# Feed-forward part of a gated cross-attention block: two unit tiles of the next batch beside each token tile of this one

## The chip, the cores and the metric
The kernel runs on one core of a Trainium2 chip, on five engines with queues of their own: TensorE (PE, and PEld for its weight loads), VectorE (DVE), ScalarE (ACT), GpSimd (POOL) and SyncE (SP), which issues the transfers. Each engine works through its queue in order; the queues meet only at semaphores. The metric is the device time of one launch in microseconds, lower is better, as the median of several runs.

## The reference, cut to what matters
There are 4 batches of 1024 tokens with 512 features. After a gated cross-attention (unchanged here) comes a gated feed-forward part:

```
x = x + tanh(g_ffn) * ffn(layernorm(x))

h = bit_linear(x, w1)            # 512 -> 2048 hidden units
h = depthwise_conv1d(h)          # three taps along the tokens, per unit
h = silu(h + conv_b)
y = bit_linear(h, w2)            # 2048 -> 512

bit_linear(x, w): xq = round(x * 127 / max|x|) / scale, one scale per token, over all its features
                  wq = ternary weights;  return xq @ wq.T
```

What matters for the order of the work: the rounding before the second product needs the largest |h| of a token over all 2048 units. So no token of a batch can go on to the second product before all units of that batch are done. The convolution, the other way round, needs neighbouring tokens of one unit.

## The kernel before, in words
The sizes: a batch has NT = 8 token tiles of 128 tokens, and KH = 16 unit tiles of 128 hidden units. The first product is made with units on the partitions and 1024 tokens along the row; the second with tokens on the partitions. PSUM has 8 banks of 512 words; a unit tile takes two of them (a pair), a turned unit tile two more (banks 6 and 7).

For unit tile n (counted through the batches), these steps run; the letters are used in the rest of this document:
- F(n): 8 matmuls of the first product (`pe_first`, L1745) into a pair of banks.
- g(n): VectorE multiplies the pair in place by the tokens' scales (`dve_scaled`, L1263).
- t(n), u(n): ScalarE writes the middle tap with its bias (L1008) and the last tap (L1012), both from the pair (`taps`).
- c(n): VectorE adds the first tap, from the pair (`first_tap`, L1489). The pair is free after it.
- tap(n): GpSimd adds the last tap (L819).
- C(n): 8 transposes to tokens on the partitions, into banks 6 and 7 (`turn_units`, L1889).
- silu(n): ScalarE writes the activated unit tile from there into `hT`, a tile of 8 tokens by 2048 units in fp32 that holds one batch (L1045).
- max(n): VectorE takes the largest value of each token (`biggest`, L1494).

When the 16 unit tiles of a batch are done, five small VectorE operations give the scales (`unit_scales`, L1498 to L1505). Then for token tile m:
- VectorE rounds it in place, by adding a large constant (`round_up`, L1511 and L1513); ScalarE subtracts the constant into bf16 (`integers`, L1018 and L1023).
- T(m): 16 transposes (`turn_h`, L1876) into two banks; ScalarE copies them out (`turned_units`, L1054 for halves, L1030 for a whole one).
- S(m): 16 matmuls of the second product (`second`, L1902).
- o(m): VectorE scales the result and adds it to x (`add_out`, L1518); SyncE stores it.

So each batch has a stage of units and then a stage of token tiles. Only the first few unit tiles of the next batch are begun within the token stage: F, g and the taps for four of them. Three pairs of banks rotate among the unit tiles, and two of them are lent to the token stage (`PAIR`, `out_bank`, `turned_bank`). The order is written out by hand in four loops, one per engine, and the waits count named events (`D_DVE`, `D_ACT`).

In the gaps stands a second chain: the layernorm and rounding of the last batch's x, done by VectorE in the token stages of batches 0 and 1 (`ln_steps`, from L1072 to L1125), with one ScalarE square root (L824), and the transposes and the row of scales for batches 2 and 3 (`ln_turn`, L1594; `ln_row`, L1580).

Of the kernel before, what the change touches and what calls it, by code (L numbers as in the profile page):

```python
# [18 lines left out]
F32 = mybir.dt.float32  # L19
# [6 lines left out]
P = 128  # L26
# [17 lines left out]
def flamingo_gated_block(nc, x, ctxT, mask, mask_cols, g_x, g_f, wsT, bk_cols, b_v, wtT, bq_cols, woT, b_out,  # L44
# [13 lines left out]
    with ExitStack() as ctx:  # L58
# [156 lines left out]
        hT = sb("hT", [P, NT, HID], F32)  # L215
# [27 lines left out]
        hsc = sb("hsc", [P, NT], F32)  # L243
        hdq = sb("hdq", [P, NT], F32)
# [87 lines left out]
        pool_tap = sem("pool_tap")  # L332
        pe_ct = sem("pe_ct")
# [70 lines left out]
        PAIR = [[j % 3 for j in range(KH)]]  # L404
        for b in range(1, B):
            first_three = PAIR[b - 1][KH - 3:]
            PAIR.append([first_three[j] if j < 3 else first_three[(j - 4) % 3] for j in range(KH)])

        def pair(b, j):
            return ps[:, 2 * PAIR[b][j]:2 * PAIR[b][j] + 2, :].rearrange("p a t -> p (a t)")  # L410

        def out_bank(b, i):
            return 2 * PAIR[b][KH - 3] + i % 2

        def turned_bank(b, i):
# [18 lines left out]
        def counts(names):  # L434
# [8 lines left out]
        LN_DVE, LN_DVE_N = counts([f"stat{i}" for i in range(NT)] + [f"aggr{i}" for i in range(NT)] + ["rstd"]  # L443
                                  + [f"ln{i}" for i in range(NT)] + [f"am{i}" for i in range(NT)]
                                  + ["amc", "rec", "asc", "adq"]
                                  + [f"{w}{i}" for i in range(NT) for w in ("xr", "xi")])
        LN_ACT, LN_ACT_N = counts(["row"] + [f"xT{i}" for i in range(NT // 2)])
        names = ["g0_0", "g0_1"]
        for b in range(B):
            for j in range(KH):  # L450
                if b == 0 or j >= 3:
                    names.append(f"c{b}_{j}")
                if j >= 2:
                    names.append(f"hmax{b}_{j - 2}")
                if j + 2 >= KH and b + 1 < B:
                    names.append(f"g{b + 1}_{j + 2 - KH}")
                elif j + 2 < KH and (b == 0 or j + 2 >= 4):
                    names.append(f"g{b}_{j + 2}")
            names += [f"hmax{b}_{KH - 2}"] + ([f"c{b + 1}_0", f"g{b + 1}_2"] if b + 1 < B else []) + [f"hmax{b}_{KH - 1}"]
            names += [f"{w}{b}" for w in ("hm", "hmc", "hrec", "hsc", "hdq")]  # L460
            names += [f"sc{b}_0a", f"sc{b}_0", f"sc{b}_1"] + ([f"c{b + 1}_1"] if b + 1 < B else [])
            names += [f"sc{b}_2"] + ([f"c{b + 1}_2"] if b + 1 < B else [])
            for i in range(NT):
                if i + 3 < NT:
                    names.append(f"sc{b}_{i + 3}")
                if i == NT - 1 and b + 1 < B:
                    names.append(f"g{b + 1}_3")
                names.append(f"o{b}_{i}")
        D_DVE, _ = counts(names)
        names = ["t0_0", "u0_0", "t0_1", "u0_1"]  # L470
        for b in range(B):
            for j in range(KH):
                if j + 2 >= KH and b + 1 < B:
                    names += [f"t{b + 1}_{j + 2 - KH}", f"u{b + 1}_{j + 2 - KH}"]
                elif j + 2 < KH and (b == 0 or j + 2 >= 3):
                    names += [f"t{b}_{j + 2}", f"u{b}_{j + 2}"]
                names.append(f"silu{b}_{j}")
            if b + 1 < B:
                names += [f"t{b + 1}_2", f"u{b + 1}_2"]
            names += [f"sub{b}_0a", f"sub{b}_0", f"hT{b}_0a"]  # L480
            for i in range(NT):
                if i + 1 < NT:
                    names.append(f"sub{b}_{i + 1}")
                names.append(f"hT{b}_{i}")
        D_ACT, _ = counts(names)

# [34 lines left out]
        def _(sp):  # L521
# [262 lines left out]
        def _(pool):  # L784
# [41 lines left out]
        def act_ln_row(act, b):  # L826
# [1152 lines left out]
```

## Time and profile before

| what | value |
|---|---|
| median of 3 runs | 1693.51 us (1690.1 to 1697.37) |
| the profiled execution's own time | 1691.95 us |
| its span, first to last instruction | 1690.1 us |
| TensorE, share of the span | 94% |
| VectorE | 67% |
| ScalarE | 51% |
| GpSimd | 43% |
| mean granted clock of TensorE | 0.982 |

The span is what the rows below are counted in; the run's own time is 1.85 us longer. The shares are means over stages that differ: attention fills the time to about 1285 us, the feed-forward part what follows. Times of rows are microseconds from the start of the span. Consecutive operations of one engine overlap by about a tenth of a microsecond at their ends, so the start-to-start distance is what an operation costs its engine, and the printed duration is what an operation on another engine waits for.

### The profile page before, as it was taken

How to read it: one execution, taken by the hardware profiler on the slowest of the kernel's cores; microseconds unless marked ns; L12 is line 12 of the kernel's file. 1: busy time of each engine (PE TensorE's matmuls, PEld its weight loads, DVE VectorE, ACT ScalarE, POOL GpSimd, SP SyncE). 2: the span in 40 equal slices, each digit the busy share in tenths (PEclk: the TensorE clock that was granted, in tenths of full speed). 3: DMA queues.
4: the chain of work that ended last, by engine and by line, in shares of the span. 5: the costliest groups of instructions: out<-in, count | busy, mean ns of one | idle time of the engine just before them, and what ended most of it. 6: DMA issues, size and time to landing. Idle time of an engine off the chain costs nothing. (4 is left out here: it accounts for less than half of the span.)

```text
span 1690.1 us, 23527 instructions
## 1 busy us (share of the span) xinstructions
PE 1592.1 (94%) x8370; PEld 1001.8 (59%) x8370; DVE 1130.5 (67%) x2237; ACT 856.5 (51%) x974; POOL 725.2 (43%) x314
## 2 busy tenths in 40 slices
PE   6899999999999999999999999999999798897968
PEld 5788878888886644555445544554455454454534
DVE  7777636444444767766776687667537959969493
ACT  3233323333331254433665265526657978879676
POOL 1231000000000099974987588857944605336160
PEclk9999999999999999999999999999999999998989
DMA  7787656555534352222333133213244020110202
GB/s 259 268 273 256 213 184 232 212 187 192 192 141 172 120 206 76 76 88 83 119 126 113 64 138 126 101 54 110 89 150 150 1 82 13 47 54 7 94 1 82
DMA packets 116408, 217.67 MB, mean 129 GB/s; under 512 B 10056, under 2 KB 35656, under 8 KB 116304
## 3 DMA queue, kind: packets, MB, share of 16 engines
q1 hardware_dynamic: 116304, 216.31, 36.6%
q8 instruction: 62, 1.02, 0.3%
q14 instruction: 42, 0.34, 0.1%
HBM read 133.16 MB, written 83.12 MB: 128 GB/s over the span
## 5 line engine op out<-in xcount | busy, mean ns | idle before, releaser
L812 POOL TENSOR_TENSOR acc<-acc,pr 128x1024 f32<-128x1024 f32 x188 | 448.7, 2387 | 92.7 <-ACT pr L842 71.8
L842 ACT ACTIVATE pr<-ps,mcol 128x1024 f32<-128x1024 f32 x256 | 275.1, 1114 | 317.0 <-PE ps L1639 316.6
L1140 DVE CUSTOM_DVE_ANT_0 junk<-ps,mbias 128x512 bf16<-128x512 f32 x512 | 332.6, 688 | 105.3 <-PE ps L1612 105.1
L1651 PE MATMUL ps<-pr,vv 128*64 128x512 f32 x1024 | 261.0, 608 | 0.0
L819 POOL TENSOR_TENSOR h_first<-h_first,last_tap 128x1023 f32<-128x1023 f32 x43 | 105.3, 2450 | 174.8 <-DVE h_first L1489 144.2
L1612 PE MATMUL ps<-kh,qh 64*128 64x512 f32 x512 | 150.2, 471 | 5.2 <-DVE nmv L1140 4.4
L1612 PEld LDWEIGHTS ps<-kh,qh 64*128 64x128 f32 x512 | 68.4, 184 | 139.3 <-issue 56.3
L793 POOL MEMSET nmt<- 128x128 f32 x1 | 0.2, 205 | 344.0 <-DVE chl L1375 344.0
L1745 PE MATMUL ps<-xiT,w1q 128*128 128x512 bf16 x512 | 121.2, 380 | 2.7 <-DVE x2t L1518 2.7
L1902 PE MATMUL ps<-w2q,hq 128*128 128x512 bf16 x512 | 121.9, 392 | 2.0 <-ACT hq L1030 1.3
L812 POOL TENSOR_TENSOR acc<-pr 128x1024 f32<-128x1024 f32 x32 | 76.7, 2396 | 105.3 <-ACT pr L842 105.3
L1651 PEld LDWEIGHTS ps<-pr,vv 128*64 128x64 f32 x1024 | 60.2, 135 | 95.1 <-issue 88.0
L1639 PE MATMUL ps<-qh,kd_hi 64*128 64x512 f32 x512 | 103.9, 397 | 0.0
L1567 PE MATMUL ps<-chh,wsh 128*128 128x512 f32 x256 | 101.7, 397 | 1.7 <-DVE chl L1375 1.7
L1639 PE MATMUL ps<-qh,kl 64*128 64x512 f32 x512 | 102.4, 391 | 0.0
L1639 PE MATMUL ps<-ql,kd_hi 64*128 64x512 f32 x512 | 102.4, 391 | 0.0
L1567 PE MATMUL ps<-wsh,chh 128*128 128x512 f32 x256 | 101.2, 395 | 0.3 <-DVE cst L1433 0.3
L1569 PE MATMUL ps<-chh,wsl 128*128 128x512 f32 x256 | 100.7, 393 | 0.0
L1568 PE MATMUL ps<-chl,wsh 128*128 128x512 f32 x256 | 100.6, 393 | 0.0
L1568 PE MATMUL ps<-wsl,chh 128*128 128x512 f32 x256 | 99.7, 389 | 0.0
L1569 PE MATMUL ps<-wsh,chl 128*128 128x512 f32 x256 | 99.7, 389 | 0.0
L984 ACT ACTIVATE vst<-vf,maskc 128x512 f32<-128x512 f32 x32 | 23.2, 725 | 125.8 <-DVE vf L1411 96.5
(181 smaller groups left out, 3141.9 us busy)
## 6 DMA issues: line engine op xcount, KB each, us to landing
craw<-in_ctxT SPq DMA_DIRECT2D x8, 2048.0 KB, 8.8
xa<-in_x SPq DMA_DIRECT2D x32, 256.0 KB, 3.8
wraw<-in_w1T SPq DMA_DIRECT2D x16, 512.0 KB, 5.9
wraw<-in_w2T SPq DMA_DIRECT2D x16, 512.0 KB, 6.8
q_split<-kqh SPq DMA_DIRECT2D x32, 256.0 KB, 2.0
q_split<-kql SPq DMA_DIRECT2D x32, 256.0 KB, 2.3
base<-lna SPq DMA_DIRECT2D x32, 256.0 KB, 4.0
k_split<-kqh SPq DMA_DIRECT2D x32, 256.0 KB, 2.0
```

Source lines behind the costliest of these rows:

```text
L812: nc.gpsimd.tensor_tensor(acc[:, blk % 2, :], first, pr[:, (8 * blk + j) % NP, :], ALU.add).then_inc(pool_acc, 1)
L819: nc.gpsimd.tensor_tensor(h[tile(b, j)][:, 0:S - 1], h[tile(b, j)][:, 0:S - 1], last_tap[j % 2][:, 0:S - 1], ALU.add).then_inc(pool_tap, 1)
L842: act.activation(pr[:, u % NP, :], ps[:, 2 * (u % 2):2 * (u % 2) + 2, :].rearrange("p a t -> p (a t)"), ACT.Exp, bias=mcol[:, (u // 64) * ...
L1140: dve.tensor_tensor_reduce(out=(junk1 if n < LEAD and n % 2 else junk)[:, e, :], in0=ps[:, first_bank(n) + e, :], in1=mbias[:, b % 2, kk * ...
L1567: pe.matmul(acc, lh, rh, start=k == 0, stop=False)
L1568: pe.matmul(acc, lh, rl, start=False, stop=False)
L1569: last = pe.matmul(acc, ll, rh, start=False, stop=k == n - 1)
L1612: last = pe.matmul(ps[:, first_bank(n) + e, :], qh[g % 3][64 * e:64 * e + 64, i * P:(i + 1) * P], kh[g % 3][64 * e:64 * e + 64, kk * CH:(k ...
L1639: last = pe.matmul(ps[:, 2 * (u % 2) + e, :], of_keys[64 * e:64 * e + 64, :], of_tokens[64 * e:64 * e + 64, :], start=j < 2 and w == 0, st ...
L1651: last = pe.matmul(ps[64 * e:64 * e + 64, 6 + blk % 2, :], vv[g % 2][:, j, 64 * e:64 * e + 64], pr[:, u % NP, e * CH:(e + 1) * CH], start= ...
L1745: last = pe.matmul(ps[:, 2 * PAIR[b][j] + t, :], w1q[:, k, j * P:(j + 1) * P], xiT[b % 2][:, k, t * 512:(t + 1) * 512], start=k == 0, stop ...
L1902: last = pe.matmul(ps[:, out_bank(b, i), :], hq[:, i % 2, j, :], w2q[:, j, :], start=j == 0, stop=j == KH - 1)
```

## The change
The two stages are merged into one order of steps. Step m (from -1 to 31) makes, beside token tile m of one batch, two unit tiles of the next batch: F, g, the taps and c of units 2m+20 and 2m+21, and C, silu and max of units 2m+18 and 2m+19. It also rounds tile m+2 and turns tile m+1. Batch 0's 16 unit tiles are made as before. Steps -1 to 21 begin two unit tiles each, step 22 only finishes two, steps 23 to 31 hold token tiles alone. Where a step's next tile is the first one of a batch (m = -1, 7, 15, 23), the scales come at the step's head and the tile is rounded in two halves.

What else differs:
- `hT` gets a layout of cells; a unit tile of the next batch takes the cells of the token tile just rounded off. So silu(n) waits for GpSimd's subtraction of that tile.
- The rounding moves from VectorE to ScalarE, and the subtraction from ScalarE to GpSimd.
- Bank 4 holds half a turned tile, bank 5 the second product, two pairs (banks 0 to 3) serve the unit tiles, where there were three. A tile is turned in two halves T0 and T1 through one bank: ScalarE copies the first out (ha), VectorE the second (hb).
- The last batch's layernorm: statistics by VectorE at the end of attention, the square root before the first silu, the normalisation and the rounding by GpSimd (steps 0 to 3 and 6 to 9), the maxima by VectorE (steps 1 to 4).
- The transposes for batches 2 and 3 go through bank 5 after o(m), in steps 0 to 3 and 9 to 12; batch 3's row in halves, in steps 7 and 8.

The diff, cut to its core:

```diff
-        hT = sb("hT", [P, NT, HID], F32)
+        hT = sb("hT", [P, 2, NT, NT, P], F32)
...
+        def pair_bank(n):
+            return 2 * (n % 3) if n < KH else 2 - 2 * (n % 2)
+        TURN_BANK, OUT_BANK = 4, 5
+        def unit_cells(n):
+            b, j = n // KH, n % KH
+            return hT[:, j % 2, :, j // 2, :] if b % 2 else hT[:, j % 2, j // 2, :, :]
+        def token_cells(m):
+            b, i = m // NT, m % NT
+            return (hT[:, :, i, :, :] if b % 2 else hT[:, :, :, i, :]).rearrange("p h q t -> p q h t")
...
+            def take_off(m):
+                pool.wait_ge(act_d, D_ACT[f"r{m}"])
+                if m >= 2:
+                    pool.wait_ge(pe_ht, 2 * m - 2)
+                nc.gpsimd.tensor_scalar(int_cells(m), token_cells(m), MAGIC, None, ALU.subtract).then_inc(pool_sub, 1)
...
+            for m in range(-1, TILE_N):                      # GpSimd
+                last = m % NT == NT - 1 and m + 1 < TILE_N
+                if last:
+                    take_off_halves(m + 1)
+                if m == -1:
+                    tap(KH + 1)
+                if 2 * m + 20 < UNIT_N:
+                    tap(2 * m + 20)
+                if m + 2 < TILE_N and (m + 2) % NT:
+                    take_off(m + 2)
+                if 2 * m + 21 < UNIT_N:
+                    tap(2 * m + 21)
+                if 0 <= m < NT // 2:
+                    last_norm(2 * m)
+                    last_norm(2 * m + 1)
+                if 6 <= m < 6 + NT // 2:
+                    last_integers(2 * (m - 6))
+                    last_integers(2 * (m - 6) + 1)
...
+            def silu(n):
+                act.wait_ge(pe_ct, n + 1)
+                if n >= KH:
+                    act.wait_ge(pool_sub, SUBS[freed(n)])
+                act.activation(unit_cells(n), ps[:, 6:8, :].rearrange("p a (i t) -> p (a i) t", t=P), ACT.Silu).then_inc(act_d, 1)
+            def round_up(m):
+                act.wait_ge(dve_d, D_DVE[f"hsc{m // NT}"])
+                act.activation(token_cells(m), token_cells(m), ACT.Identity, bias=magic, scale=scale_of(m)).then_inc(act_d, 1)
+            def first_half(m):
+                act.wait_ge(pe_ht, 2 * m + 1)
...
+            for m in range(-1, TILE_N):                      # ScalarE (the last batch's norm left out)
+                n = 2 * m + 20
+                last = m % NT == NT - 1 and m + 1 < TILE_N
+                if last:
+                    round_halves(m + 1)
+                if n < UNIT_N:
+                    taps(n)
+                if n - 2 < UNIT_N:
+                    silu(n - 2)
+                if m == -1:
+                    act_ln_row(act, B - 2)
+                if last:
+                    round_up(m + 2)
+                if m + 1 < TILE_N:
+                    first_half(m + 1)
+                if not last and m + 2 < TILE_N and (m + 2) % NT:
+                    round_up(m + 2)
+                if n + 1 < UNIT_N:
+                    taps(n + 1)
+                if n - 1 < UNIT_N:
+                    silu(n - 1)
...
+            for m in range(-1, TILE_N):                      # VectorE
+                n = 2 * m + 20
+                if m % NT == NT - 1 and m + 1 < TILE_N:
+                    biggest(n - 3)
+                    unit_scales((m + 1) // NT)
+                if m == -1:
+                    first_tap(n - 1)
+                    dve_diagonal(dve, B - 2)
+                if n < UNIT_N:
+                    dve_scaled(dve, n)
+                if m % NT != NT - 1 and n - 3 < UNIT_N:
+                    biggest(n - 3)
+                if n < UNIT_N:
+                    first_tap(n)
+                if n - 2 < UNIT_N:
+                    biggest(n - 2)
+                if n + 1 < UNIT_N:
+                    dve_scaled(dve, n + 1)
+                if m >= 0:
+                    add_out(m)
+                if m + 1 < TILE_N:
+                    second_half(m + 1)
+                if n + 1 < UNIT_N:
+                    first_tap(n + 1)
+                if 1 <= m < 1 + NT // 2:
+                    dve_last_max(dve, 2 * m - 2)
+                    dve_last_max(dve, 2 * m - 1)
+                if m == 1 + NT // 2:
+                    dve_last_scales(dve)
+                if m == 6:
+                    dve_diagonal(dve, B - 1)
...
         def pe_first(pe, n):
+            if n >= 3:
+                back = n - 3 if n <= KH else n - 2
+                pe.wait_ge(dve_d, D_DVE[f"c{back}"])
+                pe.wait_ge(act_d, D_ACT[f"u{back}"])
...
+            for m in range(-1, TILE_N):                      # TensorE
+                n = 2 * m + 20
+                if n < UNIT_N:
+                    pe_first(pe, n)
+                if m == -1:
+                    ln_row(pe, B - 2)
+                if n - 2 < UNIT_N:
+                    turn_units(n - 2)
+                if m + 1 < TILE_N and m % NT != NT - 1:
+                    turn_h(m + 1, 0)
+                if n + 1 < UNIT_N:
+                    pe_first(pe, n + 1)
+                if m >= 0:
+                    second(m, 0)
+                    second(m, 1)
+                if m + 1 < TILE_N and m % NT == NT - 1:
+                    turn_h(m + 1, 0)
+                if n - 1 < UNIT_N:
+                    turn_units(n - 1)
+                if m + 1 < TILE_N:
+                    turn_h(m + 1, 1)
+                if m in LN_AT:
+                    kind, b, u = LN_AT[m]
+                    pe.wait_ge(dve_d, D_DVE[f"o{m}"])
...
```

In the changed code T0 waits for hb of the tile before (one bank for turned halves), T1 for ha, the second half of S for hb, and S(m) for o(m-1) (one output bank).

## Rows read from the trace of the kernel before

**Rows 1.** The page, part 1: busy time, share, instructions.
```profile
PE 1592.1 (94%) x8370; PEld 1001.8 (59%) x8370; DVE 1130.5 (67%) x2237; ACT 856.5 (51%) x974; POOL 725.2 (43%) x314
```

**Rows 2.** The chain that ended last: start, length; first c after each token stage.
```profile
1399.96 1.27 DVE h_first L1489
...
1499.91 1.27 DVE h_third L1489
```

**Rows 3.** Busy time by stretch, batch 1's unit stage: PE, PEld, DVE, ACT, POOL, clock.
```profile
1400.00:1450.00 50.00, 39.85 (x223) 21.68 (x221) 49.93 (x46) 45.78 (x45) 33.02 (x14) 0.99 0.00 1
```

**Rows 4.** Timeline, two unit tiles of batch 1: start, length, engine, line.
```profile
1402.70 1.03 ACT L1045 ACTIVATE hT<-ps 128x1024 f32<-128x1024 f32 x1
...
1403.60 1.23 ACT L1008 ACTIVATE h_first<-ps,convb,convw 128x1024 f32<-128x1024 f32 x1
...
1404.69 1.14 ACT L1012 ACTIVATE last_tap<-ps,convw 128x1023 f32<-128x1023 f32 x1
...
1405.69 1.06 ACT L1045 ACTIVATE hT<-ps 128x1024 f32<-128x1024 f32 x1
1405.73 1.22 DVE L1263 TENSOR_TENSOR ps<-ps,row 128x1024 f32<-128x1024 f32 x1
1406.86 1.27 DVE L1489 SCALAR_TENSOR_TENSOR h_first<-ps,convw,h_first 128x1023 f32<-128x1023 f32 x1
1406.98 1.21 ACT L1008 ACTIVATE h_first<-ps,convb,convw 128x1024 f32<-128x1024 f32 x1 [0.23 <-DVE ps L1263]
...
1408.05 1.21 DVE L1494 TENSOR_REDUCE hmax<-hT 128x8 f32<-128x1024 f32 x1
...
1408.21 2.35 POOL L819 TENSOR_TENSOR h_first<-h_first,last_tap 128x1023 f32<-128x1023 f32 x1 [1.09 <-ACT h_first L1008]
...
1409.17 1.22 DVE L1263 TENSOR_TENSOR ps<-ps,row 128x1024 f32<-128x1024 f32 x1
```

**Rows 5.** Timeline of PE, end of batch 1's token stage.
```profile
1485.35 1.06 PE L1876 MATMUL ps<-identb,hi 128*128 128x128 bf16 x16
1486.25 3.62 PE L1902 MATMUL ps<-w2q,hq 128*128 128x512 bf16 x16
1489.70 1.89 PE L1745 MATMUL ps<-xiT,w1q 128*128 128x512 bf16 x8
1491.43 1.04 PE L1889 MATMUL ps<-ident,h_third 128*128 128x128 f32 x8
1492.30 3.62 PE L1902 MATMUL ps<-w2q,hq 128*128 128x512 bf16 x16
```

**Rows 6.** Timeline, last token stage: a second product, its addition, and the last addition.
```profile
1657.93 3.62 PE L1902 MATMUL ps<-w2q,hq 128*128 128x512 bf16 x16
...
1661.66 0.75 DVE L1518 SCALAR_TENSOR_TENSOR x2t<-ps,hdq,x2t 128x512 f32<-128x512 f32 x1 [2.40 <-PE ps L1902]
...
1686.85 0.75 DVE L1518 SCALAR_TENSOR_TENSOR x2t<-ps,hdq,x2t 128x512 f32<-128x512 f32 x1 [2.70 <-PE ps L1902]
```

**Rows 7.** Timeline of DVE, end of batch 0's unit stage, and a diagonal.
```profile
1335.62 1.28 DVE L1489 SCALAR_TENSOR_TENSOR h_first<-ps,convw,h_first 128x1023 f32<-128x1023 f32 x1
...
1342.51 1.22 DVE L1494 TENSOR_REDUCE hmax<-hT 128x8 f32<-128x1024 f32 x1
...
1344.62 0.17 DVE L1504 TENSOR_SCALAR hsc<-hsc 128x8 f32<-128x8 f32 x1
...
1351.07 2.19 DVE L1079 TENSOR_TENSOR diag<-ident,adq 128x1024 f32<-128x1024 f32 x1
```

**Rows 8.** Groups by line and form: count, busy us, mean ns, idle before.
```profile
L1023 ACT ACTIVATE hi<-hT 128x2048 bf16<-128x2048 f32 x28 | 53.4, 1909 | 2.4 <-DVE hT L1513 2.4
L1054 ACT ACTIVATE hq<-ps 128x1024 bf16<-128x1024 bf16 x8 | 8.2, 1020 | 0.7 <-PE ps L1876 0.7
L1107 DVE TENSOR_REDUCE amax<-xn 128x1 f32<-128x512 f32 x8 | 4.9, 675 | 0.0
```

**Rows 9.** The same view, GpSimd's one-input operation from the weight split.
```profile
L788 POOL CAST wsh<-wstage 128x1024 fp32r<-128x1024 f32 x8 | 11.2, 1401 | 82.5 <-DMA wstage<-in_wsT 82.5
```

More of the change, by code:

```diff
@@ L469, in flamingo_gated_block @@
-        D_DVE, _ = counts(names)
[L470 to L484, printed above, removed]
+        LN_LAST, _ = counts(["row0", "row1"] + [f"xT{i}" for i in range(NT // 2)])
@@ new lines, in flamingo_gated_block, with ln_done @@
+        LN_LAST = {name: (B - 1) * LN_ACT_N + at for name, at in LN_LAST.items()}
+        LN_POOL, _ = counts([f"{w}{i}" for i in range(NT) for w in ("off", "ln")] + [f"{w}{i}" for i in range(NT) for w in ("xr", "xi")])
+        LN_AT = {m: ("turn", B - 2, m) for m in range(NT // 2)} | {7: ("row", B - 1, 0), 8: ("row", B - 1, 1)} \
+            | {9 + u: ("turn", B - 1, u) for u in range(NT // 2)}
+        def ln_done(m):
+            kind, b, u = LN_AT[m]
+            if b == B - 2:
+                return b * LN_ACT_N + LN_ACT[f"xT{u}"]
+            return LN_LAST[f"row{u}" if kind == "row" else f"xT{u}"]
@@ L485, in flamingo_gated_block @@
         D_ACT, _ = counts(names)
+        SUBS, _ = counts([part for m in range(TILE_N) for part in (([("e", m)] if m % NT == 0 else []) + [("s", m)])])
         w1_flat = w1T.rearrange("d (a c) -> (d a) c", c=1024)
@@ new lines, in _ @@
+            for n in range(KH + 1):
+                tap(n)
+            for m in range(-1, TILE_N):
[16 more added lines that the diff above has]
+                    last_integers(2 * (m - 6) + 1)
@@ L1001, in _, with taps @@
             c_act(act)
[L1003 to L1005 removed]
+            def taps(n):
+                act.wait_ge(dve_d, D_DVE[f"g{n}"])
                 if n >= 3:
                     act.wait_ge(pe_ct, n - 2)
[L1008 to L1009 removed]
+                j = n % KH
+                act.activation(h[n % 3], pair(n), ACT.Identity, bias=convb[:, j:j + 1], scale=convw[:, j, 1:2]).then_inc(act_d, 1)
@@ L1025, in turned_units @@
[L1025 to L1034 removed]
+                act.activation(last_tap[n % 2][:, 0:S - 1], pair(n)[:, 1:S], ACT.Copy, scale=convw[:, j, 2:3]).then_inc(act_d, 1)
@@ L1035, in _ @@
+            taps(0)
+            taps(1)
             act_ln_row(act, 1)
@@ L1069, in ln_stat @@
-        def ln_stat(dve, b, i):
-            if i == 0:
-                dve.wait_ge(sp_xn_in, 16)
-            dve.bn_stats(st2[:, i, :], xn[:, i, :]).then_inc(dve_ln, 1)
+            act_ln_std(act)
+            for n in range(KH):
+                if n < KH - 2:
+                    taps(n + 2)
+                silu(n)
+                if n >= KH - 2:
+                    taps(n + 2)
+            for m in range(-1, TILE_N):
+                n = 2 * m + 20
+                last = m % NT == NT - 1 and m + 1 < TILE_N
+                if m - 1 in LN_AT:
+                    kind, b, u = LN_AT[m - 1]
+                    if kind == "row":
+                        act_ln_half_row(act, u)
+                    else:
+                        act_ln_turned(act, b, u)
+                if m == 6:
+                    act.wait_ge(dve_ln, LN_DVE["rec"])
+                    act.activation(asc[:], asc[:], ACT.Copy, scale=127.0).then_inc(act_sc, 1)
+                    act.activation(adq[:, B - 1, :], amax[:], ACT.Copy, scale=deq1).then_inc(act_sc, 1)
+                if last:
+                    round_halves(m + 1)
[5 more added lines that the diff above has]
+                    act_ln_row(act, B - 2)
+                if last:
+                    round_up(m + 2)
+                if m + 1 < TILE_N:
+                    first_half(m + 1)
+                if not last and m + 2 < TILE_N and (m + 2) % NT:
+                    round_up(m + 2)
[3 more added lines that the diff above has]
+                    silu(n - 1)
```

541 lines of the change are left out of this document (242 added, 299 removed).

## The prediction
> **What bounds the kernel now.** I read the page's shares first, then the chain that ended last, then the stretches, then the timeline of single tiles. The shares make TensorE the bound at 94% [rows 1]. That is a mean over attention and the feed-forward part. In the chain, the first c after batch 1's and batch 2's begin lie at 1399.96 and 1499.91 [rows 2], so a batch takes 99.95 us. In the 50 us of batch 1's unit stage VectorE is busy for 49.93 and TensorE for 39.85 [rows 3]: the units are VectorE's. In the timeline one unit tile lasts from g at 1405.73 to the next g at 1409.17, 3.44 us, and VectorE has no gap in it [rows 4]. In the token stage the bound is TensorE: 0.90 for the transposes (1485.35 to 1486.25) and 3.45 for the second product, 4.35 us per tile [rows 5]. TensorE's own work for a batch is 16 x (1.73 + 0.87) + 8 x 4.35 = 76.4 us. So 23.5 us of each 99.95 are idle TensorE, and that is what merging the stages can reach.
>
> **One merged step, engine by engine.** Costs are start-to-start distances.
> - TensorE: two F (1.73), two C (0.87), T0 and T1 (0.90 together), S (3.45) [rows 5]: 9.55 us.
> - VectorE: two units of 3.44 [rows 4], o and hb. o has 0.75 [rows 6], of which 0.08 overlap: 0.67. hb copies 1024 bf16 elements from PSUM; nothing in the trace is that. g, 1024 elements from PSUM, has 1.22 [rows 4]; o, 512 from PSUM, has 0.75 [rows 6]. I take g's, its element count, less the overlap: 1.14. Sum 8.7.
> - ScalarE: silu 0.90, t 1.09, u 1.00 [rows 4], twice: 5.98. ha 0.90 (1.02 less overlap). The rounding r reads and writes 2048 elements; the subtraction of the same size has 1.909 [rows 8], and t, which takes scale and bias per partition as r does, has 0.18 more than silu, which doesn't [rows 4]. So r is 2.1, start to start 1.99. The ends: 1.91, the subtraction's own, and 2.4, twice t. Sum 8.9.
> - GpSimd: two taps of 2.35 [rows 4] and the take-off of 2048 elements with one input. Nearest is the cast, 1024 elements and one input, 1.401 [rows 9]: twice that is 2.8, which I take. The tap is the upper end: two inputs, 2.35 for 1023, so 4.7. The lower end is 2.0, from ScalarE's copy of 1024 (1.02) [rows 8] as a rate that GpSimd has not shown. Sum 7.5.
>
> [...]
>
> **But no engine sets the step; a loop through three of them does.** Only two pairs of banks are left, VectorE's queue is in order, and c(n) must wait for ScalarE's u(n). I follow it with a hand-over of 0.07, as between c's end at 1408.13 and the tap at 1408.21, and 1.25 from g's start to t's (1405.73 to 1406.98) [rows 4]:
> c(n) to max 1.19, max to g(n+1) 1.12, g to t 1.25, t to u 1.09, u to c(n+1) 1.17, c to g(n+2) 1.19, g to t 1.25, t to u 1.09, u to c(n+2) 1.17. That is 10.52 us for two units. ScalarE's own way from u(n) to t(n+1) is silu 1.00, ha 0.90, r 0.90, then 1.99: 4.79, against 4.73 through VectorE. So 10.6 us. I then laid the other queues against it. C(n) waits for silu(n-1), since banks 6 and 7 are shared; then T0, F(n+3), S(m+1), C(n+1), T1 follow, and hb finds T1 ready 1 us before c(n+3) is due. The take-off ends about 1 us before TensorE asks for T0. F(n+3), which must wait for c(n+1) now that there are two pairs, still starts in time. TensorE idles 1 us per step; what is late is u.
>
> **The sum, from c(15) of batch 0 at 1335.62 [rows 7].** Until there nothing moves: the added statistics (8 at about 0.85) fall into VectorE's waits for the projection, and the square root in front of silu(0) takes one of ScalarE's.
> 1. To t(20), step 0: 25.4. F(17) waits for c(15), so g(17) comes 1 us late; max(15) starts near 1342.4, as at 1342.51 before, and scales are out 2.28 later (1344.62 + 0.17) [rows 7]. Then c(17) 1.19, the diagonal 2.19 [rows 7], g(18), and ScalarE's t, u, silu(16), row, r(1), ha(0), t, u in a line until 1358.6, c(19), g(20).
> 2. Steps 0 to 6: 7 x 10.6 = 74.2. Eight maxima (675 ns) [rows 8] stand between c and the next g, on the loop: 5.0. The scales 0.4, the diagonal 2.1. Sum 81.7. The turns for batch 2 stand in TensorE's idle 1 us. GpSimd has four operations of 512 more: 4 x 0.7, together 10.3, just under the step.
> 3. Steps 7 to 21: 15 x 10.6 = 159. At m = 7 and 15 the scales stand before g, and ScalarE rounds two halves before t: t comes 4.6 us after the last max begins where 1.2 is normal, so 3.4 each. Half rows 1. Sum 166.8.
> 4. Step 22 and the hand-over to batch 3's tiles: max(63), scales, two halves on ScalarE and GpSimd (1.4 each), T0, ha, T1, hb, to T0(25): 15.7. Nothing hides it.
> 5. Steps 24 to 30, tiles alone. Two loops. TensorE and VectorE: T0 0.45, S to o 3.73 (1657.93 to 1661.66) [rows 6], o 0.67, hb 1.22 and a hand-over: 6.1. ScalarE and GpSimd: T0 to ha 0.68, ha 0.90, r and hand-over 2.18, take-off 2.8, hand-over 0.06: 6.6. The second is longer: six of them, 39.6. Before, a tile took 4.35. So seven tiles get slower by 2.25 each: one output bank, one turning bank and a longer chain where TensorE used to be the only limit.
> 6. From T0(31): 0.45 + 3.73 + 0.67 + 1.28 + 3.73 and the 3.25 that follow the last addition (1686.85 to 1690.1) [rows 6]: 13.1.
>
> Sum 342.3 us, against 354.5 from 1335.62 to the span's end: 12 us less. The span becomes 1678, the profiled run's own time 1680 (1691.95 - 12.2). The median of the runs shown lies 1.6 above the profiled run; I predict 1680, nearer to the latter. A batch's period falls from 99.95 to 8 x 10.6 + 3.4 = 88; three of them win over 30 us, of which the start (1) and the end (4, 5) take more than half back.
>
> [...]
>
> **Rivals.**
> - A, the forecast: the loop of 10.6. 1680, alone 1670 to 1687. Chance 0.52.
> - B, TensorE sets the step at 9.55. For it: all other sums are below. Against it: the hand-overs in [rows 4] are measured and leave c(n) no earlier place. 22 x 1.05 = 23 less: 1657. Chance 0.06.
> - C, the loop slips. ScalarE's 4.79 is already level with VectorE's 4.73, and ha and silu each wait for TensorE in ScalarE's queue, with t(n+1) queued behind them, and VectorE waits for t. If r costs 2.4, or T0 comes late because the take-off did, 0.6 per step goes straight into the loop: 22 x 0.6 = 13, and 1693, no change. Chance 0.22.
> - D, GpSimd becomes the bound, slower than before. The take-off at a two-input operation's 4.7: the tile-only loop is 8.5 instead of 6.6, 11 more; the halves in 4, 2 more; in the eight steps with the last batch's norm GpSimd has 4.7 + 4.7 + 4.8 = 14.2 against 10.6 (11.9 where the maxima stand), 25 more; elsewhere 3. Together 41: 1721. It decides from 3.5 us per take-off, where the gain is gone. For it: ScalarE needed 1.909 for the same subtraction, and the tap has shown GpSimd at twice VectorE's time for c (2.35 against 1.19) [rows 4]. Against: the cast's 1.401. Chance 0.15.
> - Something that I have not seen: 0.05, on the slow side.
>
> **How the numbers follow.** 0.5%, 8.5 us, is about what a measurement of this kernel can tell from no change. Faster (below 1685): most of A, and B: 0.60. Same (1685 to 1702): C and A's upper end: 0.22. Slower: D, the unseen and C's end: 0.18. The range leaves out B's lower and D's upper part: 1663 to 1704.
>
> **What would show it.** The distance between silu(n-2) and silu(n) in steps 8 to 14: 10.6 for A, 9.6 for B, over 11 for C. VectorE idle before L1489 on ScalarE's u, twice a step (new; there was none). The take-off's mean: 2.8, or above 3.5 for D. The start-to-start distance of second products in the last eight tiles: 6.6, set by GpSimd. TensorE's share of a merged step: 90%. The forecast is wrong if the step is not within 0.4 of 10.6, or the tiles at the end not within 0.6 of 6.6.

## The result and the profile after

The changed kernel takes 1748.62 us (1745.48 to 1753.64), the kernel before 1694.3 (1690.1 to 1697.37). The ratio is 1.0325, 95% interval 1.0292 to 1.0359: slower by 3.3%, where 1680 was forecast. Its span is 1746.5 us, 68.5 more than the 1678 of the sum.

The page of the changed kernel, part 1, against [rows 1]:

```profile
PE 1602.2 (92%) x8336; PEld 1011.6 (58%) x8370; DVE 1108.9 (63%) x2207; ACT 833.7 (48%) x972; POOL 932.7 (53%) x382
```

GpSimd has 207.5 us more work than before. 53% of the span still looks harmless; but the last 400 us, from 1346.5 on, hold 325.9 us of GpSimd's work. The stretches show it (busy time of PE, PEld, DVE, ACT and POOL, then the granted clock, the DMA share and GB/s):

```profile
1400.00:1450.00 50.00, 36.58 (x205) 20.12 (x206) 29.39 (x30) 30.02 (x26) 49.63 (x20) 0.83 0.09 32
1600.00:1650.00 50.00, 45.27 (x295) 26.59 (x296) 38.14 (x37) 42.64 (x39) 45.77 (x15) 1.00 0.12 43
1650.00:1700.00 50.00, 29.66 (x165) 16.26 (x167) 12.01 (x18) 18.89 (x15) 28.74 (x8) 0.80 0.17 53
1700.00:1746.00 46.00, 27.42 (x154) 13.61 (x154) 7.49 (x11) 10.03 (x7) 20.53 (x4) 0.89 0.15 52
```

Where [rows 3] had VectorE at 49.93 of 50, GpSimd is now at 49.63 and VectorE at 29.39. In the steps without the norm (the second line) GpSimd has 45.77 of 50 and TensorE 45.27. In the last tiles nobody is full: a chain.

GpSimd's operations in the feed-forward part, by line and form (count, busy us, mean ns, idle before and its releaser):

```profile
L868 POOL TENSOR_SCALAR hi<-hT 128x2048 bf16<-128x2048 f32 x28 | 150.2, 5365 | 24.5 <-ACT hT L1133 24.0
...
L875 POOL TENSOR_SCALAR hi<-hT 128x1024 bf16<-128x1024 f32 x8 | 23.0, 2886 | 12.8 <-ACT hT L1128 12.8
L883 POOL TENSOR_SCALAR xn<-xn,rs 128x512 f32<-128x512 f32 x8 | 12.5, 1568 | 0.8
L881 POOL TENSOR_SCALAR xn<-xn,mv 128x512 f32<-128x512 f32 x8 | 12.5, 1566 | 0.0
L892 POOL TENSOR_SCALAR xi<-xn 128x512 bf16<-128x512 f32 x8 | 11.9, 1488 | 0.7
L890 POOL TENSOR_SCALAR xn<-xn,asc 128x512 f32<-128x512 f32 x8 | 5.5, 694 | 0.0
```

L868 is the take-off: 5.37 us, where 2.8 was taken and 4.7 was the upper end. Of the norm's four operations three take 1.49 to 1.57 us and one, L890, 0.694. L890 is the only one with two operators, a multiplication and an addition; the others subtract or multiply once. That odd row is where the experiments begin.

GpSimd's timeline in one step with the norm (start, length), from one take-off to the next:

```profile
1386.35 5.37 POOL L868 TENSOR_SCALAR hi<-hT 128x2048 bf16<-128x2048 f32 x1
1391.68 2.35 POOL L862 TENSOR_TENSOR h_third<-h_third,last_tap 128x1023 f32<-128x1023 f32 x1
1394.01 1.57 POOL L881 TENSOR_SCALAR xn<-xn,mv 128x512 f32<-128x512 f32 x1
1395.67 1.57 POOL L883 TENSOR_SCALAR xn<-xn,rs 128x512 f32<-128x512 f32 x1
1397.21 1.57 POOL L881 TENSOR_SCALAR xn<-xn,mv 128x512 f32<-128x512 f32 x1
1398.87 1.57 POOL L883 TENSOR_SCALAR xn<-xn,rs 128x512 f32<-128x512 f32 x1
1400.40 2.36 POOL L862 TENSOR_TENSOR h_first<-h_first,last_tap 128x1023 f32<-128x1023 f32 x1
1402.73 5.38 POOL L868 TENSOR_SCALAR hi<-hT 128x2048 bf16<-128x2048 f32 x1
```

No gap: 2 x 2.36 + 5.37 + 4 x 1.57 = 16.4 us (with the overlaps 16.38 from one take-off to the next) is the step. In the last tiles the take-offs begin 9.3 us apart on average (1680.41 to 1726.98, five distances), where [rows 5] had 4.35 a tile. Two of them with what stands between (the bracket is idle time and its releaser):

```profile
1680.41 5.36 POOL L868 TENSOR_SCALAR hi<-hT 128x2048 bf16<-128x2048 f32 x1 [4.21 <-ACT hT L1133]
...
1685.84 0.62 PE L1958 MATMUL ps<-identb,hi 128*128 128x128 bf16 x8 [2.52 <-POOL hi L868]
...
1686.49 1.02 ACT L1139 ACTIVATE hq<-ps 128x1024 bf16<-128x1024 bf16 x1 [6.16 <-PE ps L1958]
1687.41 2.08 ACT L1133 ACTIVATE hT<-hT,cst,hsc 128x2048 f32<-128x2048 f32 x1
...
1689.58 5.36 POOL L868 TENSOR_SCALAR hi<-hT 128x2048 bf16<-128x2048 f32 x1 [3.80 <-ACT hT L1133]
```

It is the loop that the prediction named (take-off, T0, ha, r, take-off), at 5.43 + 0.65 + 0.92 + 2.17 = 9.17. Three of the six distances from 1670.84 on are 9.16 or 9.17; the other three are 9.50 to 9.58, and there T0 takes 0.96 to 1.03 us instead of 0.62.

### The profile page after: what moved, and what is told of

The parts are those of the page before. It is cut to its first block and busy times, and to the rows that moved or that the text cites. A ratio compares the mean times of both kernels' runs of the same rounds, so it can differ in the third digit from the quotient of the medians.

```text
span 1746.5 us, 23636 instructions
## 1 busy us (share of the span) xinstructions
PE 1602.2 (92%) x8336; PEld 1011.6 (58%) x8370; DVE 1108.9 (63%) x2207; ACT 833.7 (48%) x972; POOL 932.7 (53%) x382
## 5 line engine op out<-in xcount | busy, mean ns | idle before, releaser
L868 POOL TENSOR_SCALAR hi<-hT 128x2048 bf16<-128x2048 f32 x28 | 150.2, 5365 | 24.5 <-ACT hT L1133 24.0
L1829 PE MATMUL ps<-xiT,w1q 128*128 128x512 bf16 x483 | 126.4, 406 | 5.0 <-DVE h_first L1574 3.2
L1958 PE MATMUL ps<-identb,hi 128*128 128x128 bf16 x512 | 45.4, 240 | 83.5 <-POOL hi L868 63.3
```

The source lines that it names most:

```text
L868: nc.gpsimd.tensor_scalar(int_cells(m), token_cells(m), MAGIC, None, ALU.subtract).then_inc(pool_sub, 1)
L1829: last = pe.matmul(ps[:, pair_bank(n) + t, :], w1q[:, k, j * P:(j + 1) * P], xiT[b % 2][:, k, t * 512:(t + 1) * 512], start=k == 0, stop=k ...
```

## The experiments

Four questions: why GpSimd's operations cost what they do; how much of the loss hangs on that; what closes the merged step once GpSimd is cheap; what the last tiles cost by themselves. All changes are to the changed kernel. Unless said otherwise times are medians beside the kernel before on the same chip (1692.5 to 1693.1).

### Does the number of operators set GpSimd's price?

Three kernels. `e1_two_op_all` gives each one-operator operation a neutral second operator, `e2_two_op_takeoff` the take-off alone, `e3_two_op_norm` the norm's alone.

```diff
-nc.gpsimd.tensor_scalar(int_cells(m), token_cells(m), MAGIC, None, ALU.subtract)
+nc.gpsimd.tensor_scalar(int_cells(m), token_cells(m), MAGIC, 1.0, ALU.subtract, ALU.mult)     # e1, e2
...
-nc.gpsimd.tensor_scalar(xn[:, i, :], xn[:, i, :], rs2[:, 1, i:i + 1], None, ALU.mult)
+nc.gpsimd.tensor_scalar(xn[:, i, :], xn[:, i, :], rs2[:, 1, i:i + 1], 0.0, ALU.mult, ALU.add)  # e1, e3
```

> The changed kernel with every one-operator tensor_scalar of GpSimd given a second operator that changes nothing (times 1, plus 0); same data, layout, waits. In the changed kernel's trace GpSimd's two-operator form of 512 elements (L890) takes 694 ns, its one-operator forms of 512 take 1488 to 1568, and the take-off of 2048 takes 5365. Theory A (the operator count sets GpSimd's rate, and all else goes as forecast): take-off about 4 x 0.69 = 2.8 us or a little less, a merged step about 10.6, the last tiles 6.2 to 6.6 apart, time about 1680. Rival B (the take-off is slow because of its size, its cells or its bf16 output): it stays at 5.4, time 1725 or above, since only the norm's operations get faster. Rival C (the merged order itself loses, in waits between the engines, whatever GpSimd costs): take-off 2.8, but steps stay at 10.9 to 16 and the time above 1720.

> Only the take-off of token tiles gets the second operator; the last batch's norm keeps its one-operator forms. It splits the excess of the changed kernel. Theory A: the last eight tiles go from 9.3 apart to 6.2 to 6.6 (18 us less), the steps with the norm from 16.4 and 14.5 to about 13.7 and 12 (some 20 less), the first steps 5 less: about 1705. Rival B (the take-off's layout is the cause): no change, 1748. If the norm alone were the loss: less than 10 us gained.

> Only the last batch's normalisation and rounding on GpSimd get the second operator; the take-off stays as it is, 5.37 us. Theory A: four steps from 16.4 to about 12.9, four from 14.5 to about 12.3 (23 us less), the end unchanged at 9.3 per tile: about 1725. If the steps' excess comes from elsewhere (the maxima on VectorE, the turns through the one output bank): less than 8 us gained, above 1738.

Measured: 1799.07 (ratio 1.0634, 1.0608 to 1.0659); 1800.65 (1795.41 to 1804.58 without one execution of 5378 us, ratio 1.0641); 1748.21 (ratio 1.0332, 1.0309 to 1.0355). All three miss what was expected (about 1680, 1705 and 1725). The theory of the operator count is wrong, and the groups of the first kernel say how:

```profile
L868 POOL TENSOR_SCALAR hi<-hT 128x2048 bf16<-128x2048 f32 x28 | 198.4, 7085 | 24.2 <-ACT hT L1133 24.0
...
L881 POOL TENSOR_SCALAR xn<-xn,mv 128x512 f32<-128x512 f32 x8 | 16.0, 1997 | 0.0
L892 POOL TENSOR_SCALAR xi<-xn 128x512 bf16<-128x512 f32 x8 | 15.4, 1922 | 0.7
L890 POOL TENSOR_SCALAR xn<-xn,asc 128x512 f32<-128x512 f32 x8 | 5.5, 693 | 0.0
L883 POOL TENSOR_SCALAR xn<-xn,rs 128x512 f32<-128x512 f32 x8 | 5.5, 693 | 0.8
```

Subtract and multiply is dearer than subtract alone (7.09 against 5.37, 2.00 against 1.57). L883, now multiply and add, falls from 1.57 to 0.69, as L890. In the third kernel gains and losses cancel: L881 and L892 lose 0.43 and 0.44 each, L883 gains 0.88. So its unchanged time doesn't speak for a cause outside GpSimd, as its expectation would have it: GpSimd's work in these steps is the same. And with the take-off dearer by 1.72 (28 of them and 8 halves of 0.86: 55 us) the kernel takes 50 to 52 us more: nearly all of it lies on the path.

### The price by itself

`e4_bench` is the changed kernel with fifteen GpSimd operations behind its last take-off; the result of the kernel isn't touched.

```diff
+            for w in (512, 1024, 2048):
+                a, b = xf[:, 0:w], xf[:, 2048:2048 + w]
+                trial(lambda: nc.gpsimd.tensor_scalar(b, a, 1.5, None, ALU.subtract))            # L927
+                trial(lambda: nc.gpsimd.tensor_scalar(b, a, 1.5, None, ALU.mult))                # L928
+                trial(lambda: nc.gpsimd.tensor_scalar(b, a, 1.5, 1.0, ALU.subtract, ALU.mult))   # L929
+                trial(lambda: nc.gpsimd.tensor_scalar(b, a, 1.0, 1.5, ALU.mult, ALU.add))        # L930
+                trial(lambda: nc.gpsimd.tensor_copy(b, a))                                       # L931
```

> The changed kernel with 15 GpSimd operations added at the end of its queue, on scratch rows nobody reads any more: at 512, 1024 and 2048 elements in plain rows of fp32, each with a constant: subtract alone, multiply alone, subtract and multiply, multiply and add, and a copy. It measures the disputed cost by itself; its time says nothing. Theory A: the one-operator forms take about 2.6 ns per element (5.3 us at 2048), the two-operator forms about 1.2 (2.5 us) whatever the operators, the copy about 1.3 as in the weight split. Rival B: at 2048 elements all forms lie together, or one and two operators differ only where the output is bf16.

GpSimd's timeline, the operations of 512 and of 2048 elements:

```profile
1731.96 1.49 POOL L927 TENSOR_SCALAR xn<-xn 128x512 f32<-128x512 f32 x1
1733.53 1.49 POOL L928 TENSOR_SCALAR xn<-xn 128x512 f32<-128x512 f32 x1
1735.11 1.93 POOL L929 TENSOR_SCALAR xn<-xn 128x512 f32<-128x512 f32 x1
1737.12 0.62 POOL L930 TENSOR_SCALAR xn<-xn 128x512 f32<-128x512 f32 x1
1737.81 0.61 POOL L931 COPY xn<-xn 128x512 f32<-128x512 f32 x1
...
1750.16 5.37 POOL L927 TENSOR_SCALAR xn<-xn 128x2048 f32<-128x2048 f32 x1
1755.61 5.37 POOL L928 TENSOR_SCALAR xn<-xn 128x2048 f32<-128x2048 f32 x1
1761.06 7.10 POOL L929 TENSOR_SCALAR xn<-xn 128x2048 f32<-128x2048 f32 x1
1768.24 1.90 POOL L930 TENSOR_SCALAR xn<-xn 128x2048 f32<-128x2048 f32 x1
1770.20 1.89 POOL L931 COPY xn<-xn 128x2048 f32<-128x2048 f32 x1
```

From 512 to 2048 elements: one operator (5.37 - 1.49) / 1536 = 2.53 ns an element; subtract and multiply 3.37; multiply and add 0.83, the same as a copy; each beside some 0.2 us. Nothing waits between them, and the last five run when the other engines have finished (VectorE's last operation begins at 1742.88); 5.37 there, in plain rows of fp32, is what L868 takes (5.365). So neither the cells, the bf16 output nor other engines' traffic makes the price, which was rival B of the first kernel. Why multiply and add alone has the copy's rate is not shown; other pairs of operators were not run.

### The same arithmetic in the cheap form

`e5_mul_add_takeoff` writes the take-off as multiply by 1.0 and add the negative constant. `e6_mul_add_all` does so in the norm too: x times rs plus a small per-tile column, -mean x rs, which VectorE makes once; two operations of 1.57 become one.

```diff
-nc.gpsimd.tensor_scalar(int_cells(m), token_cells(m), MAGIC, None, ALU.subtract)
+nc.gpsimd.tensor_scalar(int_cells(m), token_cells(m), 1.0, -MAGIC, ALU.mult, ALU.add)     # e5, e6
...
-nc.gpsimd.tensor_scalar(xn[:, i, :], xn[:, i, :], mv2[:, i, 0:1], None, ALU.subtract)
-nc.gpsimd.tensor_scalar(xn[:, i, :], xn[:, i, :], rs2[:, 1, i:i + 1], None, ALU.mult)
+nc.gpsimd.tensor_scalar(xn[:, i, :], xn[:, i, :], rs2[:, 1, i:i + 1], nmr[:, i:i + 1], ALU.mult, ALU.add)   # e6
...
-nc.gpsimd.tensor_scalar(xi[:, i, :], xn[:, i, :], MAGIC, None, ALU.subtract)
+nc.gpsimd.tensor_scalar(xi[:, i, :], xn[:, i, :], 1.0, -MAGIC, ALU.mult, ALU.add)         # e6
```

> The take-off written as times 1 plus the negated constant, the same values; the last batch's norm stays as it is. By the measurement of GpSimd's forms alone this form takes 1.90 us for 2048 elements, against 5.37 for subtract alone. Theory A (GpSimd's price of the take-off is the loss, the step's loop is as forecast): the last tiles 5.7 to 6.2 apart instead of 9.3 (20 less), the norm's steps from 16.4 to 12.9 and from 14.5 to 11 (28 less), the first steps and the hand-overs some 8 less, merged steps 10.6 instead of 10.9: 1748 goes to about 1690. Rival C (the merged order loses by its waits): above 1720 although the take-off is at 1.9.

> As the one before, and the last batch's norm too: one multiply-add per token tile with the negated mean times the factor as the addend (made by one small VectorE operation), and the subtraction of the constant as multiply-add. GpSimd's work in the norm's steps falls to 4.7 + 1.9 + 1.4. Theory A: this is the forecast with its GpSimd prices true, steps of 10.6 throughout (11.9 where the maxima stand), last tiles 5.7 apart by ScalarE and GpSimd: span 1670, time about 1672, up to 1680. Rival C: 1700 or more, with the excess over 10.6 per step in waits between VectorE, ScalarE and TensorE. Rival B of the forecast (TensorE sets the step, 9.6): 1650.

Measured: 1685.75 (ratio 0.9963, 0.995 to 0.9976) and 1682.55 (0.994, 0.9925 to 0.9954). The take-off's form alone thus gives back 62.9 us, more than the 54.3 that the change had lost. The norm's form adds 3.2: in e5 GpSimd still sets the norm's steps at 12.9 us, in e6 they take 11.9. Rival C (above 1720, above 1700) is out for both. The first lies near its expected 1690, the second 2.6 above its expected 1672 to 1680. GpSimd's groups of e6:

```profile
L868 POOL TENSOR_SCALAR hi<-hT 128x2048 bf16<-128x2048 f32 x28 | 53.2, 1900 | 28.6 <-ACT hT L1131 27.8
...
L881 POOL TENSOR_SCALAR xn<-xn,rs,nmr 128x512 f32<-128x512 f32 x8 | 6.1, 773 | 0.0
```

So 97 us of whole-tile take-offs are gone, and the whole loss with them. The distances between the first take-offs of successive batches put it in place (start of the first half take-off, by batch, and the end of the span):

| stretch | changed kernel | e6 | difference |
|---|---|---|---|
| batch 0's tiles (norm in four steps) | 122.5 | 100.2 | 22.3 |
| batch 1's tiles (norm's rounding in the first steps) | 104.4 | 90.7 | 13.7 |
| batch 2's tiles | 89.8 | 87.6 | 2.2 |
| batch 3's tiles, alone | 81.1 | 54.0 | 27.1 |

Together 65.3 us (1746.5 - 1681.2). Where taps and take-off are GpSimd's only work, 10.1 us in a step, 5.37 costs little (the step takes 10.90 instead of 10.68); where the norm is on top, or where the take-off stands in a chain, all of it shows.

### What closes the merged step?

In e6 a merged step takes 10.68 us, against a forecast of 10.6. The prediction put VectorE's max on that loop. `e7_loop_order` moves max(n-2) behind g(n+1).

```diff
                 if n < UNIT_N:
                     first_tap(n)
-                if n - 2 < UNIT_N:
-                    biggest(n - 2)
                 if n + 1 < UNIT_N:
                     dve_scaled(dve, n + 1)
+                if n - 2 < UNIT_N:
+                    biggest(n - 2)
```

> The one before with one change of order on VectorE: max(n-2) stands behind g(n+1) instead of ahead of it. It tests the loop c, max, g, t, u, c that the forecast named as what sets the merged step. Theory A: max leaves the loop; ScalarE's queue (8.9) and the rest of the loop then set the step, 9.6 to 10.1 instead of 10.6, over 20 steps 10 to 18 us less than the kernel before it. Rival C' (the step is set elsewhere, by TensorE's transposes behind silu, or by GpSimd): no change within 3 us, or slower, as max comes later.

Measured: 1681.88 (0.994, 0.9926 to 0.9954), the same as e6, and the step is still 10.68. Theory A missed; it is what rival C' gave, though for none of its reasons. The timeline of e6 over one step, ScalarE's and VectorE's lines of the loop:

```profile
1577.27 1.21 DVE L1577 TENSOR_REDUCE hmax<-hT 128x8 f32<-128x1024 f32 x1
1577.66 2.11 ACT L1131 ACTIVATE hT<-hT,cst,hsc 128x2048 f32<-128x2048 f32 x1
1578.39 1.22 DVE L1346 TENSOR_TENSOR ps<-ps,row 128x1024 f32<-128x1024 f32 x1
...
1579.66 1.22 ACT L1109 ACTIVATE h_first<-ps,convb,convw 128x1024 f32<-128x1024 f32 x1
...
1581.98 1.28 DVE L1572 SCALAR_TENSOR_TENSOR h_first<-ps,convw,h_first 128x1023 f32<-128x1023 f32 x1 [0.98 <-ACT last_tap L1112]
...
1583.18 1.22 DVE L1346 TENSOR_TENSOR ps<-ps,row 128x1024 f32<-128x1024 f32 x1
...
1584.43 1.21 ACT L1109 ACTIVATE h_first<-ps,convb,convw 128x1024 f32<-128x1024 f32 x1 [1.65 <-DVE ps L1346]
```

t(n+1) at 1579.66 follows r without a gap (ScalarE is never idle before it), and g had begun 1.27 before, as it must: both branches arrive together. In this half of the step ScalarE's queue (t, u, silu, ha, r: 5.9) and VectorE's (t, u, c, max, g: 5.9) are equal; the prediction had that (4.79 against 4.73 from u on) and I then shortened one of two. In e7 g begins right behind c, and t(n+1) still follows r without a gap, 5.90 after t(n). In the other half ScalarE is idle for 1.65. So two more kernels, with the last tiles as in the next experiment: `e9_round_late` moves ScalarE's r to the end of the step, one token tile earlier, and `e10_both_late` has e7's order besides.

```diff
                 if m + 1 < TILE_N:
                     first_half(m + 1)
-                if not last and m + 1 < ALONE and m + 2 < TILE_N and (m + 2) % NT:
-                    round_up(m + 2)
                 if n + 1 < UNIT_N:
                     taps(n + 1)
                 if n - 1 < UNIT_N:
                     silu(n - 1)
+                if m + 1 < ALONE and ahead:       # ahead = m + 3 < TILE_N and m % NT not in (5, 6)
+                    round_up(m + 3)
```

> The kernel with the multiply-add take-off and norm and the two pairs of banks for the last seven tiles (1673.2), with ScalarE's rounding r moved from the slot between ha(m+1) and t(n+1) to the end of the step, one token tile earlier (r(m+3) after silu(n-1), where ScalarE was idle 1.65 us before t). Theory, as the two traces of the merged step now read: between t(n) and t(n+1) two branches of equal length, ScalarE's (t, u, silu, ha, r: 5.9) and VectorE's (t, u, c, max, g: 5.9). Cutting ScalarE's alone leaves VectorE's: the step stays at 10.5 to 10.7, time 1671 to 1675. Rival: ScalarE's queue alone is what binds: the step falls to 9.7, time about 1660.

> The same, and VectorE's maximum of unit n-2 behind g(n+1) as well. Theory of two equal branches: both are cut, first half t to t 2.31 + 1.20 + 1.26 = 4.8, second half ScalarE's t, u, silu, r = 5.0, step 9.8 (TensorE's own work is 9.55); 15 steps by 0.8 and seven with the maxima by up to 0.8 less: 1655 to 1663. Rival: the order of TensorE's queue, with C(n) waiting for silu(n-1), holds the step above 10.3: 1667 to 1673.

Measured: 1679.27 (1677.05 to 1681.61; ratio 0.9919, 0.9902 to 0.9936) and 1656.84 (1655.31 to 1662.35; 0.9794, 0.9774 to 0.9815). Their base, e8 below, is 1673.18. e9 is outside its expected 1671 to 1675. Cutting ScalarE's branch alone makes the plain step 10.89, not 10.5 to 10.7: VectorE's 5.9 stays in the first half, and r now stands in the second, where t, u, silu, r take 5.0 instead of 4.78. Cutting both makes it 9.76, and e10 is where it was expected. That holds for the plain steps. In steps 9 to 12 ScalarE also copies the turned x of batch 3 in the second half: there a step takes 10.68 in e8, 11.8 in e9 and 10.68 in e10, so cutting both gains nothing in these four. ScalarE in e10, one step from t to t to t:

```profile
1562.16 1.21 ACT L1119 ACTIVATE h_third<-ps,convb,convw 128x1024 f32<-128x1024 f32 x1
...
1566.93 1.21 ACT L1119 ACTIVATE h_first<-ps,convb,convw 128x1024 f32<-128x1024 f32 x1 [0.73 <-DVE ps L1359]
...
1569.93 2.11 ACT L1141 ACTIVATE hT<-hT,cst,hsc 128x2048 f32<-128x2048 f32 x1
...
1571.91 1.21 ACT L1119 ACTIVATE h_first<-ps,convb,convw 128x1024 f32<-128x1024 f32 x1
```

4.77 through VectorE and 4.98 through ScalarE's queue. From t(18) to t(63) e8 takes 260.7 us, e9 267.1 and e10 245.5. Each order alone gave nothing or lost; both gave 16.3 us, all but 1 or 2 of them in the merged steps, which is what shows that the branches were equal. TensorE is busy for 47.39 of 50 us in this stretch (e10, 1560 to 1610), so its own 9.55 is next.

### The last tiles

`e8_tail_banks` is e6 with the last seven token tiles alternating between two turning banks (4 and 2) and two output banks (5 and 3), free by then, and with r(m+2) ahead of ha(m+1) there.

```diff
+        def turn_bank_of(m):
+            return 2 if m >= ALONE and m % 2 else TURN_BANK        # ALONE = 25
+        def out_bank_of(m):
+            return 3 if m >= ALONE and m % 2 else OUT_BANK
...
+                if m + 1 >= ALONE and m + 2 < TILE_N:     # ScalarE, at the head of the step
+                    round_up(m + 2)
...
-                    if m:
-                        pe.wait_ge(dve_d, D_DVE[f"hb{m - 1}"])
+                    elif m:
+                        pe.wait_ge(dve_d, D_DVE[f"hb{m - 1 - (m > ALONE)}"])
```

> The multiply-add kernel (without the order change) with the last seven token tiles using the four banks that the unit tiles have left: turned halves in banks 4 and 2 by turns, the second product in 5 and 3 by turns, and ScalarE rounding tile m+2 ahead of copying tile m+1. It measures what the end costs for its single banks and its chain. Theory A: 5.7 per tile falls to TensorE's 4.4 to 4.8, 7 to 9 us less. If the end is bound by TensorE at a lower granted clock already: less than 3.

Measured: 1673.18 (1671.92 to 1673.85; 0.9881, 0.9865 to 0.9897), 9.4 less than e6, where 7 to 9 were expected. TensorE in its last tiles:

```profile
1643.42 3.62 PE L2001 MATMUL ps<-w2q,hq 128*128 128x512 bf16 x16
...
1646.88 1.06 PE L1973 MATMUL ps<-identb,hi 128*128 128x128 bf16 x16
1647.77 3.62 PE L2001 MATMUL ps<-w2q,hq 128*128 128x512 bf16 x16
```

4.35 us a tile, TensorE's 0.90 + 3.45, as in [rows 5]; e6 has 5.70 there. So what was left of the tail's loss was the chain through one bank of each kind and ScalarE's order; the two were changed together and are not separated.

## Why the prediction was wrong

The step that failed is the price of GpSimd's operations: "Nearest is the cast, 1024 elements and one input, 1.401: twice that is 2.8, which I take", with the tap's 4.7 as the upper end, and 0.7 for each operation of the norm. Measured: 5.37, and 1.49 to 1.57 for three of four. The value taken and the upper end were drawn by the number of inputs. What decides is the operator: a subtraction with one input (5.37) costs more than an addition with two (2.35 for 1023 elements, so 4.7), and a cast or a copy says nothing of it. It is rival D in its mechanism, at a size outside its own bounds.

By the stages of the sum (the first row is a time, the others are distances, in the profiled runs; the number of the sum's point in brackets):

| stage | forecast | changed kernel | e6 |
|---|---|---|---|
| t(20) begins (1) | 1361.0 | 1363.9 | 1363.9 |
| t(20) to t(32), six steps (2) | 69.0 | 90.0 | 69.1 |
| t(32) to T0(25) (rest of 2, 3, 4) | 195.2 | 222.4 | 200.1 |
| T0(25) to T0(31) (5) | 39.6 | 56.1 | 35.9 |
| T0(31) to the end (6) | 13.1 | 14.1 | 12.1 |
| span | 1678 | 1746.5 | 1681.2 |

1. Up to t(20): 2.8 us late, at 1363.85 where 1335.62 + 25.4 = 1361.0 was forecast. Max(15) begins at 1344.30, not near 1342.4, since it stands behind c(16), and the scales follow it.
2. Steps 0 to 6, 10.6 plus maxima: the forecast let GpSimd have 10.3 in a norm step. It has 16.4, and GpSimd sets the step. In e6, with GpSimd cheap, a step with two maxima takes 11.87 (10.6 + 1.25 = 11.85 forecast), a plain one 10.68 (10.6). The loop's size was right.
3. Steps 7 to 21: the plain ones take 10.90 in the changed kernel. Those with the norm's rounding take 14.5 (2 x 2.36 + 5.37 + 2 x 1.49 + 2 x 0.69). The boundaries were sized too small: in e6 the distance over the boundary of m = 15 is 25.27 for two steps (1521.32 to 1546.59), and the next 11.9, together 5.1 more than plain steps, not 3.4. The one of m = 7 costs about as much.
4. Hand-over to batch 3's tiles: two halves of 2.77 at the median instead of 1.4, one behind the other, and behind them the take-off of 5.37 that T0(25) waits for.
5. Last tiles: 9.3 apart, not 6.6, by the same loop with 5.37 in the take-off's place. With 1.90 there that loop gives 5.7, and e6 has 5.70. But by the prediction's terms the other loop, TensorE's and VectorE's, would then have set 6.1; it didn't, because hb takes 0.68 there and not 1.22. The first two distances in e6 are longer (1630.36, 1637.29, 1644.33: 6.9 and 7.0), 2.6 us together.
6. The end: 1.0 longer than forecast in the changed kernel, where T0(31) and the second product behind it took 0.83 and 4.70 us, at a granted clock of 0.71 (1732.4 to 1738.2), instead of 0.62 and 3.62, and 1.0 shorter in e6, where hb runs beside the first half of the product, while the sum had 1.28 for it on the path.

With 5.7 for the last tiles the sum would have been a span of 1678 - 6 x 0.9 = 1672.6. e6 has 1681.2: 2.9 more up to t(20), 5.0 in the merged steps and the hand-over, 1.7 in the last tiles, 1.0 less at the end. So that e6, with GpSimd cheap, lands near 1680 is in part luck: the take-off is 0.9 cheaper than the forecast had it, and the other stages are longer.

Put together: D's own arithmetic with the measured prices makes a norm step 16.4, a rounding step 14.5 and a last tile 9.2, each as found; D with 4.7 and 0.7 to 1.2 gave 1721. Its test, "above 3.5 for D", named the row that decided. What I should have done is give D more than 0.15: ScalarE's 1.909 for the same subtraction, times the factor of two that the tap showed, was 3.8 already, and only a cast stood against it.

Rival C, the loop slips, showed in one of its two forms, and small. ScalarE's r took 2.095, as taken (2.1). But the prediction had the take-off end about 1 us before TensorE asks for T0, and in the changed kernel's plain steps T0 waits for it:

```profile
1632.27 0.62 PE L1958 MATMUL ps<-identb,hi 128*128 128x128 bf16 x8 [1.28 <-POOL hi L868]
```

What follows on TensorE moves with it up to T1, so hb comes late, and in every other step c behind hb too: such a step takes 11.04, the others 10.70. In e6 T0 doesn't wait there and every plain step is 10.68. Rival B, 9.55 by TensorE, was ruled out by the hand-overs as they were ordered; e10's plain step comes within 0.2 of it by another order.

The prediction took 1.14 for hb, hidden in the merged steps. It takes 0.689:

```profile
L1596 DVE COPY hq<-ps 128x1024 bf16<-128x1024 bf16 x32 | 22.0, 689 | 23.3 <-PE ps L1958 23.2
```

With the take-off at 5.37 that changes nothing. In e6's last tiles it does: the take-off ends at 1651.93 and hb at 1651.81, and T0 follows both.

```profile
1650.03 1.90 POOL L868 TENSOR_SCALAR hi<-hT 128x2048 bf16<-128x2048 f32 x1 [3.80 <-ACT hT L1131]
...
1651.13 0.68 DVE L1594 COPY hq<-ps 128x1024 bf16<-128x1024 bf16 x1
...
1651.98 0.62 PE L1959 MATMUL ps<-identb,hi 128*128 128x128 bf16 x8 [1.18 <-POOL hi L868]
```

The change's idea, to fill TensorE's idle time in the unit stage, did not fail. With the take-off in its cheap form the merged order is 0.4 to 0.6% faster than the kernel before, with two free banks at the end 1.2%, with both branches of the loop cut 2.1%.

## What to carry to other kernels

Before work moves to an engine that has not done it in the trace, price that very form (operators and all) in a few instructions at the end of a queue: fifteen of them here told where 54 us of loss came from. Where two branches of a loop arrive within a tenth of a microsecond of each other, cut both or expect nothing: here, at 5.9 and 5.9, one order alone gained 0.7 us (e7) or lost 6.1 (e9), and both gained 16.3 (e10). An engine's share over the span says little about a stretch in which it gets extra work (GpSimd had 53% of the span and all of the 16.4 us of a norm step): add up its queue for each kind of step.

## What the runs showed of the hardware

In `e4_bench`, from 512 to 2048 elements of fp32, GpSimd's tensor_scalar had three rates: 0.83 ns an element for multiply and add, as for a copy; 2.53 for subtract or multiply alone; 3.37 for subtract and multiply. At 2048 elements a second operator made the operation 2.8 times faster (5.37 to 1.90) or a third slower (5.37 to 7.10). The output in bf16 changed neither of the two forms that had it: 5.365 at L868 of the changed kernel against 5.37 in the bench, 1.900 at L868 of e6 against 1.90. At 512 elements an operand per partition in a constant's place cost 0.07 us and two cost 0.15: multiply and add took 0.69 with one (L890), 0.77 with two (L881 of e6) and 0.62 with constants (the bench).

TensorE's granted clock was 1.00 in the changed kernel's plain steps (1600 to 1650), and 0.83, 0.80 and 0.89 in the other three stretches shown. In the last tiles it can be read for single operations. The T0 at 1685.84, 1704.50 and 1713.66 take 0.62 us each, at a granted clock of 1.00; those at 1676.26, 1694.99 and 1722.83 take 1.03, 0.96 and 1.03, at 0.50, 0.60 and 0.50. TensorE had been idle for 2.52, 3.31 and 2.96 us before the first three and for 2.14, 4.64 and 4.64 before the others; what lowered the clock is not shown. T0 stands in the loop of the last tiles, so the lower clock costs 0.3 to 0.4 us in three of its six distances, 1.1 us in all. What it costs in the norm's steps is not separated from the waits themselves; over the span the clock was 0.972 in the changed kernel and 0.987 in e5.
